# A gated delta-rule layer: pair mask, key norms and output factor on GpSimd instead of VectorE, and a new order of the steps

## What is computed

```
mixed = silu(causal_conv(hidden @ w_qkv, conv_w));  q, k, v = split(mixed)
z = hidden @ w_z;  beta = sigmoid(hidden @ w_b)
g = -exp(A_log) * softplus(hidden @ w_a + dt_bias)
qf = q * rsqrt(sum(q*q) + 1e-6) * 128 ** -0.5
kf = k * rsqrt(sum(k*k) + 1e-6)
def step(state, (q_t, k_t, v_t, g_t, b_t)):
    state = state * exp(g_t)
    delta = (v_t - k_t @ state) * b_t
    state = state + outer(k_t, delta)
    return state, q_t @ state
o = outs * silu(z)
o = o * rsqrt(mean(o*o) + 1e-6) * norm_gamma
x = layernorm(x + o @ w_out)
x = layernorm(x + moe(x))        # 8 experts, 2 of them a token, and a shared one
```

## Time and profile before

| | us |
|---|---|
| median of 3 runs (2553.75 to 2554.24) | 2554.12 |
| the profiled execution | 2555.36 |
| its span, first to last instruction | 2553.6 |

### The profile page before, as it was taken

The page is one execution under the profiler, slowest core; times in us unless marked ns, Lnnn a source line. Parts: engine busy times, 40 slices in busy tenths (PEclk is TensorE's granted clock), DMA queues, the critical chain, the costliest instruction groups (busy, mean ns, idle before and its releaser), DMA issues.

```text
span 2553.6 us, 57047 instructions
## 1 busy us (share of the span) xinstructions
PE 2409.7 (94%) x21614; PEld 1873.3 (73%) x21614; DVE 2017.6 (79%) x3771; ACT 1479.5 (58%) x4315; POOL 1264.3 (50%) x876
## 2 busy tenths in 40 slices
...
DMA packets 32112, 98.67 MB, mean 39 GB/s; under 512 B 4320, under 2 KB 9824, under 8 KB 31584
## 3 DMA queue, kind: packets, MB, share of 16 engines
...
## 4 chain that ended last, share of the span: by engine, by line
PE 51%; DVE 32%; issue 10%; ACT 4%; POOL 2%; DVEq 1%; POOLq 0%; DMA 0%; SPq 0%; ACTq 0%
DVE conv L1091 10%; PE bank L858 10%; PE bank L834 9%; DVE decb L1119 6%; DVE XT L1140 5%; PE bank L480 4%; PE bank L884 4%; DVE m32T L1125 3%; PE bank L933 3%; PE bank L892 3%; PE bank L898 3%; ACT og L1060 3%; DVE TT L1157 3%; PE bank L960 3%; PE bank L943 2%
## 5 line engine op out<-in xcount | busy, mean ns | idle before, releaser
L1091 DVE SCALAR_TENSOR_TENSOR conv<-bank,cw_all,conv 128x511 f32<-128x511 f32 (+2 forms) x768 | 561.9, 738 | 11.9 <-ACT conv L998 7.2
L834 PE MATMUL bank<-xT,w_kh 128*128 128x512 f32 x1024 | 540.5, 628 | 2.7 <-ACT kraw L1025 1.8
L752 POOL TENSOR_TENSOR decb<-tri_sb,bfac 128x1024 f32<-128x1024 f32 x64 | 121.4, 1897 | 850.3 <-DVE kfac L1108 809.6
L1147 DVE TENSOR_TENSOR N<-bank,lev 128x512 f16<-128x512 f32 x384 | 265.5, 691 | 297.4 <-PE bank L884 297.4
L1045 ACT ACTIVATE X<-bank 128x512 f16<-128x512 f32 x384 | 233.5, 608 | 199.7 <-PE bank L892 194.3
L858 PE MATMUL bank<-w_kh,xT 128*128 128x256 f32 x1024 | 285.2, 401 | 0.0
L975 PE MATMUL bank<-wo,ogT 128*128 128x256 f32 x1024 | 253.8, 381 | 0.0
L1048 ACT ACTIVATE XT<-bank 128x512 f16<-128x512 f32 x384 | 234.2, 610 | 0.0
L834 PEld LDWEIGHTS bank<-xT,w_kh 128*128 128x128 f32 x1024 | 160.1, 191 | 80.2 <-ACT sqj L1019 47.1
L1053 ACT ACTIVATE U<-bank 128x256 f32<-128x256 f32 x256 | 101.3, 396 | 202.6 <-PE bank L933 202.6
L975 PEld LDWEIGHTS bank<-wo,ogT 128*128 128x128 f32 x1024 | 185.9, 191 | 20.2
...
## 6 DMA issues: line engine op xcount, KB each, us to landing
...
```

The lines of the kernel that those rows point to most:

```text
L834: mm = pe.matmul(PB[j % 2][:, :], w[:, k, g * P:(g + 1) * P], xT[:, k, b * SEQ:(b + 1) * SEQ], start=(k == 0), stop=(k == KT - 1))
L1091: dve.scalar_tensor_tensor(conv[:, g, m:], PB[j % 2][:, 0:SEQ - m], cw_all[:, head, g * TAPS + 3 - m:g * TAPS + 4 - m], conv[:, g, m:], op ...
L1147: dve.tensor_tensor(blocks(N[:, i], i, 0), packed(IB[1 - i % 2], i), blocks(lev[:, 1 + i:2 + i, :], i, 0).broadcast_to(shape), ALU.mult).t ...
```

## The change

- `pairs` moves from DVE to POOL. In place of a product with a mask there are two selects: the first keeps the blocks of two, the second writes ones where the product had them. Both halves go in one piece.
- `norms` moves to POOL as `kn`: an addition, one power of 8 numbers that gives the root and the reciprocal together, and the products for `bfac` and `kfac`. It also takes the place of `nk`.
- The system is held with the opposite sign: beta is stored negative, so the masks of the levels are made positive at the start (one DVE instruction), `res` adds instead of subtracting, the sign in `u` is turned, and `mlo` has -2 on its diagonal.
- The query's norm is no longer multiplied in. It cancels in the output norm but for that norm's constant: `eq` (POOL) makes the constant of each token, and `pow` (POOL) adds it to the mean square (the 1/128 is now in `power`'s scale) ahead of its power. `qnorm`, `rqs`, `zscale` and `factor` are gone; `og` waits for the silu of z alone.
- All four lists of `ORDER` are new. `PREPARE` ties one step of the experts to `og 1` in place of `factor`.

The diff, cut:

```diff
@@ ORDER["pool"]
-        ("rqs", 0, 0), ("mlo", 0, 1), ("zscale", 0, 0), ("diag", 0, 2), ("keys", 0, 2), ("pow", 0, 0), ("ogs", 0, 0),
-        ("ogs", 1, 0), ("nk", 0, 2), ("mhi", 0, 2), ("mhi", 1, 2), ("qe", 0, 2),
+        ("pairs", 0, 1), ("keys", 0, 1), ("qe", 0, 1), ("mlo", 0, 1), ("kn", 0, 2), ("diag", 0, 2), ("pow", 0, 0),
+        ("ogs", 0, 0), ("ogs", 1, 0), ("mhi", 0, 2), ("eq", 0, 2), ("mhi", 1, 2),
@@ gates_vector
-            dve.tensor_tensor(scalars_of(Q_BETA), by_body(b_num), by_body(b_den), ALU.mult).then_inc(s_gates, 1)
+            dve.scalar_tensor_tensor(scalars_of(Q_BETA), by_body(b_num), -1.0, by_body(b_den),
+                                     op0=ALU.mult, op1=ALU.mult).then_inc(s_gates, 1)
@@ pool
-                if name == "nk":
-                    pool.wait_ge(s_ss, 2 * n + 1)
...
+                if name == "kn":
...
+                    pool.wait_ge(s_sq, 8 * n + 4)
+                    if n > 0:
+                        pool.wait_ge(s_nk, n)
+                    pool.tensor_scalar(ss[:, p], ssum[:, p, 0], 1e-6, None, ALU.add).then_inc(s_ssk, 1)
+                    pool.wait_ge(s_ssk, n + 1)
...
+                    pool.tensor_tensor(nr[:, p], ss[:, p].unsqueeze(1).broadcast_to([P, 2, CH]),
+                                       expk[:, :].unsqueeze(2).broadcast_to([P, 2, CH]), ALU.pow).then_inc(s_nk, 1)
+                    pool.wait_ge(s_nk, n + 1)
...
+                    for dst, what, done in ((bfac, Q_BETA, s_bfac), (kfac, Q_KEYS, s_kfac)):
+                        pool.tensor_tensor(by_chunk(dst[:, p]), by_chunk(scal(n, what, 0, CELLS)),
+                                           nr[:, p, 1].unsqueeze(2).broadcast_to([P, CH, VH]), ALU.mult).then_inc(done, 1)
+                elif name == "eq":
+                    pool.wait_ge(s_sq, 8 * n + 8)
+                    if n > 3:
+                        pool.wait_ge(s_mse, n - 3)
+                    pool.tensor_scalar(epsq[:, n % 4], ssum[:, p, 1], P * 1e-6, P * 1e-12, ALU.mult, ALU.add).then_inc(s_epsq, 1)
...
-                elif name == "zscale":
...
-                    pool.affine_select(out=mloT[:, :, :], in_=mloT[:, :, :], compare_op=ALU.not_equal, fill=0.0,
+                    pool.affine_select(out=mloT[:, :, :], in_=mloT[:, :, :], compare_op=ALU.not_equal, fill=-2.0,
...
+                elif name == "pairs":
+                    pool.wait_ge(s_mhi, 2 * n + 2)
+                    if n > 0:
+                        pool.wait_ge(s_new, 2 * n)
+                    pool.affine_select(out=XT[:, :, :].rearrange("p x (b j) -> p x b j", j=2),
+                                       in_=mhiT[:, :, :].rearrange("p x (b j) -> p x b j", j=2), compare_op=ALU.is_equal, fill=0.0,
+                                       base=0, pattern=[[0, CELLS], [-2, P // 2], [0, 2]], channel_multiplier=1).then_inc(s_near, 1)
+                    odd = XT[:, :, :].rearrange("p x (b j) -> p x b j", j=2)[:, :, :, 1]
+                    pool.wait_ge(s_near, n + 1)
+                    pool.affine_select(out=odd, in_=odd, compare_op=ALU.not_equal, fill=1.0,
+                                       base=-1, pattern=[[0, CELLS], [-2, P // 2]], channel_multiplier=1).then_inc(s_pair, 1)
                 elif name == "pow":
...
+                    pool.wait_ge(s_ms, 8 * n + 8)
+                    pool.wait_ge(s_epsq, n + 1)
...
+                    pool.tensor_tensor(by_chunk(ms[:, 1, :]), by_chunk(ms[:, 0, :]),
+                                       epsq[:, n % 4].unsqueeze(2).broadcast_to([P, CH, VH]), ALU.add).then_inc(s_mse, 1)
                     pool.wait_ge(s_mse, n + 1)
@@ scalar
-                        act.activation(og2[:, x, :], og[:, x, :], ACT.Square, accum_out=ms[:, 0, x:x + 1]).then_inc(s_ms, 1)
+                        act.activation(og2[:, x, :], og[:, x, :], ACT.Square, scale=P ** -0.5,
+                                       accum_out=ms[:, 0, x:x + 1]).then_inc(s_ms, 1)
@@ vector
+            far = lev[:, 1:, :].rearrange("p i n -> p (i n)")
+            dve.scalar_tensor_tensor(far, far, -1.0, far, op0=ALU.mult, op1=ALU.max).then_inc(s_lev, 1)
...
-                elif name == "norms":
...
-                elif name == "qnorm":
...
-                elif name == "pairs":
...
-                    dve.tensor_tensor(half(XT, i), half(mhiT, i), lev[:, 0, :].unsqueeze(1).broadcast_to([P, 4, P]),
-                                      ALU.mult).then_inc(s_pair, 1)
...
-                                      ALU.subtract).then_inc(s_res, 1)
+                                      ALU.add).then_inc(s_res, 1)
...
-                    dve.wait_ge(s_zq, n + 1)
+                    dve.wait_ge(s_zs, 2 * n + i + 1)
...
-                elif name == "factor":
```

More of the change, by code:

```diff
@@ L30 @@
     "tensor": [
[L31 to L40, removed]
@@ L41 @@
-        ("start", 0, 2),
+        ("vtp", 0, 1), ("join", 0, 1), ("vtp", 1, 1), ("solve", 1, 0), ("growx", 0, 1), ("gate", 0, 1),
+        ("growt", 0, 1), ("join", 1, 1), ("gate", 1, 1), ("growx", 1, 1), ("growt", 1, 1), ("write", 1, 0),
+        ("proj", 0, 2), ("proj", 1, 2), ("join", 2, 1), ("gate", 2, 1), ("read", 2, 0), ("growx", 2, 1),
+        ("out", 0, 0), ("solve", 2, 0), ("growt", 2, 1), ("join", 3, 1), ("gate", 3, 1), ("out", 1, 0),
+        ("growx", 3, 1), ("write", 2, 0), ("proj", 2, 2), ("ktp", 0, 2), ("growt", 3, 1), ("join", 4, 1),
@@ new lines @@
+        ("read", 3, 0), ("proj", 3, 2), ("growx", 4, 1), ("growt", 4, 1), ("solve", 3, 0), ("out", 2, 0),
+        ("join", 5, 1), ("out", 3, 0), ("growx", 5, 1), ("proj", 4, 2), ("growt", 5, 1), ("newton", 0, 1),
+        ("ktp", 1, 2), ("proj", 5, 2), ("newton", 1, 1), ("finish", 0, 1), ("proj", 6, 2), ("finish", 1, 1),
+        ("proj", 7, 2), ("products", 0, 2), ("solve", 0, 1), ("products", 1, 2), ("turn", 0, 0), ("write", 0, 1),
+        ("turn", 1, 0), ("project", 0, 0), ("read", 1, 1), ("project", 1, 0), ("project", 2, 0), ("start", 0, 2),
@@ L42 @@
+        ("project", 3, 0),
     ],
     "scalar": [
[L44 to L48, removed]
@@ L49 @@
-        ("turn", 1, 0), ("silu", 3, 2), ("vals", 0, 2), ("vals", 1, 2),
+        ("silu", 3, 1), ("x0", 0, 1), ("vals", 0, 1), ("vals", 1, 1), ("growx", 0, 1), ("u", 1, 0), ("growt", 0, 1),
+        ("zs", 0, 1), ("growx", 1, 1), ("growt", 1, 1), ("tap", 0, 2), ("growx", 2, 1), ("growt", 2, 1), ("zs", 1, 1),
+        ("u", 2, 0), ("silu", 0, 2), ("growx", 3, 1), ("squares", 0, 2), ("growt", 3, 1), ("tap", 1, 2),
+        ("growx", 4, 1), ("u", 3, 0), ("kraw", 0, 2), ("growt", 4, 1), ("power", 0, 0), ("growx", 5, 1),
@@ L50 @@
+        ("silu", 1, 2), ("growt", 5, 1), ("squares", 1, 2), ("power", 1, 0), ("tap", 2, 2), ("u", 0, 1),
+        ("tap", 3, 2), ("turn", 0, 0), ("silu", 2, 2), ("turn", 1, 0),
     ],
     "vector": [
-        ("conv", 0, 2), ("rhs", 2, 0), ("conv", 1, 2), ("join", 3, 1), ("conv", 2, 2), ("og", 0, 0), ("s", 2, 0),
-        ("join", 4, 1), ("rhs", 3, 0), ("conv", 3, 2), ("join", 5, 1), ("conv", 4, 2), ("norms", 0, 2),
-        ("conv", 5, 2), ("og", 1, 0), ("res", 0, 1), ("res", 1, 1), ("factor", 0, 0), ("scan", 0, 2), ("tt", 0, 1),
@@ L55 @@
[L55 to L58, removed]
+        ("conv", 0, 2), ("rhs", 2, 0), ("conv", 1, 2), ("conv", 2, 2), ("join", 3, 1), ("s", 2, 0), ("join", 4, 1),
```

84 lines of the change are left out of this document (36 added, 48 removed).

## The result

| | median us | runs | ratio to before (95%) |
|---|---|---|---|
| before | 2554.18 | 4 | 1 |
| after | 2770.03 | 4 (2766.95 to 2771.2) | 1.0843 (1.0824 to 1.0862) |

The forecast was 2472.5 us, within 2440 to 2525. The changed kernel is 8.4% slower, and lies above the price of the rival that ended on that side (2641).

A forecast was written before the change was run, and what follows sets the result against it. TensorE, 96% busy, was taken as the bound, its two waits costing 1.37 us of 35.34 a round; 0.25 saved on `TT` offset 0.25 charged, giving 33.97. 2553.6 - 85 + 3.5 = 2472, predicted 2472.5 us, range 2440 to 2525.

The forecast's parts named there:

- the rival that ended on that side: POOL's first select: runs of two cost 4 ns an element, both selects 4.8 us, 36.7 a round, 2641 us; chance 0.08.
- the small instructions' bounds: Short POOL instructions in the norms, factor and constant: 0.2 us each taken, between 0.1 and 1.0; range covers up to 0.5.
- The wait for `og`: TensorE's wait for POOL's scaled og ahead of L966, 0.49 us a body, forecast to go.
- The wait for `XT` before: TensorE's 0.88 us a body ahead of L875's transposes; about 1.6 us of DVE's second half read as waiting for POOL.
- The longer chain as a bound: Rival: POOL's small instructions up to the start cost 0.5 us each, 34.7 a round, 2517 us; chance 0.20.
- the new collision: Rival: POOL's power falls in front of a DVE scan, round 35.4 us, no change, about 2557 us; chance 0.05.
- the "floor" of the rivals: Rival: TensorE never waits, a round is 33.1 to 33.5 us; 2443 us at 33.5; chance 0.17.
- 3.5 us of loss: First two rounds, half empty: the squares, norms, decb, scan chain lies in the open, 2 x (2.4 - 0.7) = +3.5 us.
- The 0.25 us a round charged: Charge for three steps with 0.1 to 0.2 us slack and two ScalarE results 0.1 and 0.15 us late.
- the 33.1: Sum in us of TensorE's 61 steps of a round, one behind the other in the new order.

The follow-up runs named there:

- The kernel kept at the high clock: Changed kernel with three additional 128x512 f32 products on TensorE ahead of the start's wait for the pairs, that wait kept: 2647.28 us, ratio 1.0363.
- the plain select: Changed kernel with the first select given mlo's plain pattern, without runs of two, so blocks of two are left out of the inverse: 2432.17 us, ratio 0.952.
- the added wait alone: Kernel before, with one more wait: POOL begins qE only when both halves of DVE's pairs are written: 2487.2 us, ratio 0.9739.

## Why the prediction was wrong

**The step that failed** is the price of the first select. The prediction took 1.8 us for both, from the row of a plain select (L787), and named 6 as the upper bound "were the pattern's inner run to cost several times an element". Both took 5.4, the first alone 4.49 and not 1.10. The bound was right and was then not used: the range went only as far as the small instructions' bounds. And in the rival it set one shape effect that the rows do show (`qE` at 1.3 times `keys`) against a factor of four. That row was of a product; over the views where a select takes 4.48 us a product takes 1.89, so the row could say nothing of a select.

**The rival's own sum** was 36.7 us a round and 2641 us at a price of 4.8. With the measured price the same sum gives 33.97 + (5.4 - 1.8 - 0.3) = 37.3 and 2553.6 + 1.93 x 62 + 3.5 = 2677. The kernel kept at the high clock took 2647, and the rest of the forecast was pessimistic by 40 us (2432.17 with the plain select against 2472.5): 2677 - 40 = 2637, 10 us off. So the mechanism and its size were right but for the second failed step: **the sum has no term for the clock.** The earlier trace rows shows 1.00; TensorE's waits for `XT` in the full rounds of before are 0.87 us, once 1.1, and those for `og` at most 0.4. The lower clock cost 123 us: with the same wait and the clock kept high the change would have lost 93 us, not 216.

**What held.**
- The wait for `og` went: the power takes 1.64 us and not 2.49, and no scan takes more than 1.23 us, against 2.90 before.
- The small instructions on POOL cost 0.19 to 0.23 us, where 0.2 was taken. `kn` runs from 1204.20 to 1206.62, 2.4 us, as forecast.
- The wait for `XT` before was a queue, shown by the added wait alone (67 us, where 0.88 x 62 = 55 was the wait).
- The longer chain as a bound, and the new collision, did not come about. POOL's scaling of w_out, which the prediction overlooked, does stand in that chain: in one round of four it costs 1 us.

**What was too small.** With the plain select a round takes 33.51 us, the "floor" of the rivals, and not 33.97: (33.97 - 33.51) x 61 = 28 us. The third `decb` starts at 112.88 us against 116.83 before, where 3.5 us of loss were put; the stretch behind the last one is 274.5 us against 281.1, where nothing was put. Together 28 + 7.5 + 6.6 = 42, near the 40 observed. The 0.25 us a round charged for steps "with next to no slack" was not needed: with the scaling of w_out out of the way TensorE waits for none of them in the 400 us of the long stretch. The round is then 33.37 us, so the 33.1 that the prediction added up for TensorE's steps alone was 0.3 short.

**Where the gain of 129 us lies** (2554 to 2425, by the kernels measured): 67 us by the collision of the pairs with `qE`, which one wait removes; 32 more by the new order with norms and factor on POOL and w_out moved (2487 to 2455); 31 by the pairs on POOL as a product (2455 to 2425). The middle step takes in several changes at once, and their shares are not told apart. How TensorE's clock goes behind waits between 1.71 and 2.70 us was not tried.
